# A four-layer graph network on one core: four packed adjacency buffers instead of two, and a tenth of x made per chunk

## The chip, the cores and the metric

The kernel is one program on one core of a Trainium2 chip. The metric is device time in microseconds from start to end of one execution, as the median of three executions: 19903.77 us, between 19867.3 and 19942.51. The engines are called as in the profile: PE is the matmul engine and PEld its weight loads, DVE the vector engine, ACT the activation engine, POOL the gather engine, SP the queue that issues the large transfers.

## The reference, cut to what matters

The graph has 12500 nodes with 32 features and 412500 directed edges. Four graph layers follow each other, each added to its input and normalised over the features. The change touches layers 2 and 3, which are both repeated products with the same adjacency matrix:

```python
# layer 2: ten steps of personalised propagation
f = feat0 = x
for _ in range(10):
    agg = segment_sum((f * src_norm)[src], dst)      # adjacency @ f
    f = 0.9 * (agg * dst_norm) + 0.1 * feat0         # feat0 = x, ALPHA = 0.1
x = layernorm(x + f)
# layer 3: one product more
x = layernorm(x + segment_sum(x[src], dst))
```

Layer 1 (an edge network with means) runs before it, layer 4 (tensor messages on every edge) behind it.

## The kernel before

The adjacency matrix is dense and lies in HBM as small counts, two of them packed in each byte (a nibble each) in planes; `planes` says how many planes hold anything, and it is 1 here. `propagate` makes 11 passes over the matrix: passes 0 to 9 are the ten steps of layer 2, pass 10 is layer 3.

One pass has NCH = 14 chunks of output nodes, walked in pairs: `c2` counts the 7 pairs, and m = 0 or 1 is the chunk in the pair. A chunk needs HG = 7 slots of the matrix (h = 0 to 6), so a pair has SLOTS = 14 tiles (j = 0 to 13), a pass has 98, and the stage has 11 x 98 + 7 = 1085, since the load of the next pass's first chunk is also made once at the very end. Each tile takes these steps:

- SP, `load` (L1151): waits until the packed buffer is free (a count in `a_unpacked`), then issues one transfer of 784 KB into `packed[j % 2]`, one of two buffers. L1151 is the only transfer of the stage.
- DVE, `unpack` (L1287, L1288): waits for the landing and for PE to be through with the old content of slot `j % 7` (`a_used`), then writes the low and the high nibbles into the slot with two instructions.
- PE, `product` (L1206): 84 pairs of a weight load and a matmul over the slot. There are 7 slots in SBUF, so DVE can be at most one whole chunk ahead of PE.

Behind the first slot of each product (`TURN_AFTER = 1`), PE turns back the product of the chunk before (`turn_back`, L1186, 14 small matmuls) from what ACT copied out (L1246). DVE, having unpacked the 7 slots of the next chunk, adds the turned product to `agg` (`add`, L1294) and runs `finish`: `new_f` scales `agg`, adds the stored tenth of x (L1319, `tenth`, written once at L1351 before the first pass) and clears `agg` (L1322); `next_parts` then splits the new f into three bf16 parts for the next pass (L1328, L1274, L1277). Pass 9 has the shorter `finish` `into_x` (L1336), pass 10 has none.

What sets the order: SP, PE and DVE each run a `Fori` loop whose body is one pair. PE's body is written out, 2 x 588 matmuls with their weight loads and two `turn_back`s. PE has three copies of the code of a pass: even passes (source `parts[0]`), odd passes (`parts[1]`), and pass 10. In each copy the first pair is peeled off, and the other six go round the `Fori`, so the jump back to the top happens 5 times in a pass, and once more when the outer loop over two passes goes round. SP has one copy of `load_plane` for each of the 5 planes, and jumps over four of them in each pass.

`tenth` serves also as scratch for the two layer norms inside the stage (`norm(3, ...)`, `norm(4, ...)`).

Of the kernel before, what the change touches and what calls it, by code (L numbers as in the profile page):

```python
# [31 lines left out]
P = 128  # L32
# [1063 lines left out]


TURN_AFTER = 1


def propagate(nc, k, s):
# [4 lines left out]
    sb, pb, sem = k.sb, k.pb, k.sem  # L1106
    passes = STEPS + 1
    slots = [sb(f"a_slot{h}", [P, 4, HH, QW], U8, s) for h in range(HG)]
    packed = [sb(f"a_nibbles{n}", [P, 4 * PW_H], U8, s) for n in range(2)]
    parts = [sb(f"f_parts{t}", [P, NB, 3 * D], BF16, s) for t in range(2)]  # L1110
    agg = sb("agg", [P, NB, D], F32, s)
    chunk_f = sb("chunk_f", [P, CB * D], F32, s)
    chunk_zero = sb("chunk_zero", [P, CB * D], F32, s)
    tenth = sb("x_tenth", [P, NB, D], F32, s)
    norms = sb("norms", [P, NB, 2], F32, s)
    mean, var = sb("mean", [P, NB], F32, s), sb("var", [P, NB], F32, s)
    turned = sb("turned", [P, 2, CW], F32, s)
# [11 lines left out]
    with ExitStack() as q:  # L1129
        prod = [pb(f"p_prod{m}", [P, 2, 512], F32, q) for m in range(2)]  # L1130
        back = [pb(f"p_back{m}", [P, CB * D], F32, q) for m in range(2)]
        with nc.Block() as block:
# [9 lines left out]
            @block.sync  # L1142
            def _(sp):
                planes = sp.value_load(k.ctl[0:1, 1:2], min_val=1, max_val=DIGITS)
                u = sp.alloc_register("pairs_sp")
                sp.reg_mov(u, 0)

                def load(plane, chunk, n, j):

                    await_alone(sp, k.passed_sp, a_unpacked, n * SLOTS + (j + 1))  # L1150
                    sp.dma_start(view(packed[j % 2][:], 0, [[PW_H, 4], [1, PW_H]]),  # L1151
                                 slot_part(plane, chunk, j % HG)).then_inc(a_loaded[j], 16)

                def load_plane(d):
                    with sp.Fori(0, NCH // 2) as c2:
                        n = sp.snap(u, min_val=0, max_val=passes * DIGITS * NCH)
                        for j in range(SLOTS):
                            load(k.planes[d], c2 * 2 + j // HG, n, j)
                        sp.reg_add(u, u, 1)
                with sp.Fori(0, passes):  # L1160
                    load_plane(0)
                    for d in range(1, DIGITS):
                        with sp.If(planes > d):
                            load_plane(d)
                n = sp.snap(u, min_val=0, max_val=passes * DIGITS * NCH)
                for j in range(HG):
                    load(k.planes[0], 0, n, j)
                sp.wait_ge(x_ready, 1)
                sp.dma_start(k.x3_d.rearrange("(b p) f -> p b f", p=P), k.x[:]).then_inc(x_stored, 16)
                sp.wait_ge(x_stored, 16)  # L1170

            @block.tensor
            def _(pe):
# [15 lines left out]

                def product(n, m, source, p=None, turn_after=TURN_AFTER):  # L1190

                    if turn_after == 0:
                        turn_back(n, m)
                    pe.wait_ge(product_copied, n * 2 + (m + 1))
                    for h in range(HG):
                        if p is not None:
                            await_alone(pe, k.passed_pe, parts_ready, p * HG + (h + 1))
                        await_alone(pe, k.passed_pe, a_unpacked, n * SLOTS + (HG * m + h + 3))
                        for j in range(HH):
                            for r in range(3):  # L1200
                                for w in range(2):

                                    unit = (h * HH + j) * 3 + r
                                    strip = unit % 2 * 2 + (w + unit // 2) % 2
                                    rows = slice(strip * D, (strip + 1) * D)
                                    mm = nc.tensor.matmul(view(prod[m][rows, w, :], 0, [[QW, 2], [1, QW]]),  # L1206
                                                          source[:, h * HH + j, r * D:(r + 1) * D],
                                                          slots[h][:, 2 * w:2 * w + 2, j, :].bitcast(FP8),
                                                          start=(unit < STRIPS), stop=(unit >= NB * 3 - STRIPS),
                                                          tile_position=(0, strip * D))  # L1210
                        mm.then_inc(a_used, 1)
                        if h + 1 == turn_after:
                            turn_back(n, m)
# [41 lines left out]
            def _(dve):  # L1255
# [2 lines left out]
                u = dve.alloc_register("pairs_dve")  # L1258
                dve.reg_mov(u, 0)
                dve.sem_inc(taken, 3)  # L1260
                dve.sem_inc(a_unpacked, 2)
                for r in range(STRIPS):
                    nc.vector.tensor_copy(select[r * D:(r + 1) * D, :], k.ident[r * D:(r + 1) * D, r * D:(r + 1) * D])
                for d in range(DIGITS):
# [12 lines left out]
                            tt(frm, frm, to(r), ALU.subtract)  # L1277
                            dve.drain()

                def unpack(n, j, ahead=0):  # L1280

                    await_alone(dve, k.passed_dve, a_loaded[j], n * 16 + (16 + 16 * ahead))
                    await_alone(dve, k.passed_dve, a_used, n * SLOTS + (SLOTS * ahead + j + 1))
                    words = PW_H // 4
                    frm = view(packed[j % 2][:].bitcast(I32), 0, [[words, 4], [1, words]])
                    half = lambda i: view(slots[j % HG][:].bitcast(I32), i * words, [[2 * words, 4], [1, words]])
                    ts(half(0), frm, NIBBLES, None, ALU.bitwise_and)  # L1287
                    ts(half(1), frm, 4, NIBBLES, ALU.logical_shift_right, ALU.bitwise_and).then_inc(a_unpacked, 1)  # L1288
# [7 lines left out]
                def one_pass(finish):  # L1296

                    with dve.Fori(0, planes) as d:
                        with dve.Fori(0, NCH // 2) as c2:
                            n = dve.snap(u, min_val=0, max_val=passes * DIGITS * NCH)  # L1300
                            for m in range(2):
                                for h in range(HG):
                                    unpack(n, (1 - m) * HG + h, m)
                                add(n, m, c2)
                                if finish is not None:
                                    with dve.If(planes - d == 1):
                                        finish(c2 * 2 + m)
                                        if finish is not into_x and m == 1:
                                            dve.drain().then_inc(parts_ready, 1)
                            dve.reg_add(u, u, 1)  # L1310

                def new_f(c):
# [2 lines left out]
                    dve.drain()  # L1315
                    tt(view(agg[:], c * (CB * D), [[D, CB], [1, D]]), view(agg[:], c * (CB * D), [[D, CB], [1, D]]),
                       view(norms[:], c * (2 * CB), [[2, CB], [0, D]]), ALU.mult)
                    dve.drain()
                    nc.vector.scalar_tensor_tensor(chunk_f[:], part, 1.0 - ALPHA, view(tenth[:], c * (CB * D), [[1, CB * D]]),  # L1319
                                                   ALU.mult, ALU.add)  # L1320
                    dve.drain()
                    nc.vector.tensor_copy(part, chunk_zero[:])  # L1322

# [20 lines left out]

                norm(1, agg)
                for h in range(2):
                    unpack(0, h)
                ts(norms[:], k.small[:], 1.0, None, ALU.max).then_inc(norm_in, 1)
                dve.wait_ge(norm_out, 2)
                nc.vector.reciprocal(norms[:], norms[:])  # L1350
                ts(tenth[:], k.x[:], ALPHA, None, ALU.mult)  # L1351
                dve.drain()
                tt(agg[:], k.x[:], of_src, ALU.mult)
                all_parts()
                dve.drain().then_inc(parts_ready, HG)
                for h in range(2, HG):
                    unpack(0, h)
                with dve.Fori(0, STEPS // 2 - 1):
                    for odd in range(2):
                        one_pass(next_parts(parts[1 - odd]))  # L1360
                one_pass(next_parts(parts[1]))
                one_pass(into_x)
                dve.drain()
                norm(3, tenth)
                nc.vector.tensor_copy(agg[:], k.x[:])
                all_parts()
                dve.drain().then_inc(parts_ready, HG)
# [1 line left out]
                dve.drain()  # L1369
                tt(k.x[:], k.x[:], agg[:], ALU.add)  # L1370
                dve.drain()
                norm(4, tenth)
                dve.drain().then_inc(x_ready, 1)


# [420 lines left out]
```

## Time and profile before

| | us |
|---|---|
| median of three executions | 19903.77 |
| lowest, highest | 19867.3, 19942.51 |
| the profiled execution, its own time | 19936.66 |
| its span, first to last instruction | 19934.9 |
| before the adjacency stage | 8342 |
| prologue of the stage (norms, first parts) | 48 |
| passes 0 to 9 | 4603 |
| between pass 9 and pass 10 | 44 |
| pass 10 | 448 |
| behind it (layer 3's norm, layer 4) | 6449 |

All other durations in this document come from the profiled execution. In the profile's page the busy tenths of PE are at 9 in slices 17 to 26 of 40, each 498 us long; that is the adjacency stage. DVE is there at 4 to 5 tenths, the transfers at 5 tenths and 170 to 178 GB/s. In an answer on a stretch of instructions in order of time, the columns are start, duration, engine, line, operation, what it writes and reads, the count of merged instructions, and in brackets the idle time before it with what ended it; "issue" means that the engine waited for nothing that the profile shows. The DMA section lists, for each queue, packets, megabytes and the share of 16 engines' time; a queue named "instruction" carries program code to an engine's sequencer.

### The profile page before, as it was taken

What the parts mean: (1) busy time and instruction counts of PE and PEld (TensorE: products, weight loads), DVE (VectorE), ACT (ScalarE), POOL (GpSimd) and SP (SyncE); (2) the same over time, 40 slices, a digit from 0 to 9 for tenths busy, and PEclk for the clock granted to TensorE, in tenths of its full rate; (3) what the DMA queues carried; (4) which work ended last, traced back from release to release, by engine and by line L of the source; (5) the groups of instructions that cost most, each with busy time, mean ns of one, the idle gap of its engine ahead of it and who ended that gap; (6) DMA issues with size and microseconds to landing.
All of it is one profiled execution on the core that took longest, in us unless ns stands there. A gap on an engine that the chain in (4) does not pass through costs nothing. (4 is left out here: it accounts for less than half of the span.)

```text
span 19934.9 us, 398915 instructions
## 1 busy us (share of the span) xinstructions
PE 14773.5 (74%) x139606; PEld 9691.4 (49%) x139607; DVE 10952.7 (55%) x15417; ACT 5231.4 (26%) x10549; POOL 7485.0 (38%) x8530
## 2 busy tenths in 40 slices
PE   3666666666666666699999999986777777777787
PEld 2555555555555555355555555553444444444444
DVE  6444444444443444354555555446777777777777
ACT  2333333332333333000000000003444444444443
POOL 4343343433443442000000000005666666666665
PEclk8666666666666666699999999998999999999999
DMA  2010000000000000155555555551111111111111
GB/s 71 19 23 19 22 20 21 20 22 20 22 22 20 23 20 23 40 178 171 176 171 174 172 172 177 173 163 38 27 27 27 27 27 27 27 26 27 27 28 27
DMA packets 1144165, 1253.76 MB, mean 63 GB/s; under 512 B 399195, under 2 KB 1111895, under 8 KB 1142455
## 3 DMA queue, kind: packets, MB, share of 16 engines
q1 hardware_dynamic: 932547, 1124.29, 18.7%
q0 software_dynamic: 210496, 113.01, 3.9%
q8 instruction: 887, 14.53, 0.3%
q14 instruction: 235, 1.93, 0.0%
HBM read 1143.04 MB, written 93.60 MB: 62 GB/s over the span
## 5 line engine op out<-in xcount | busy, mean ns | idle before, releaser
L1458 POOL DMA_INDIRECT m_src<-x_after_layer,m_idx x3240 | 3164.0, 977 | 6734.6 <-DMA m_idx<-in_src 5620.8
L180 POOL DMA_INDIRECT l_xin<-in_x,l_idx x3240 | 3076.0, 949 | 4605.8 <-DMA l_idx<-in_src 3416.8
L1206 PE MATMUL p_prod<-a_slot,f_parts 128*32 128x448 fp8e4 x90552 | 4475.0, 360 | 418.2 <-issue 283.6
L1206 PEld LDWEIGHTS p_prod<-a_slot,f_parts 128*32 128x32 bf16 x90552 | 2460.3, 99 | 2370.3 <-issue 608.1
L581 PE MATMUL a_ps<-hot_hi,hot_lo 128*128 128x196 bf16 x6272 | 1645.0, 304 | 2122.3 <-ACT a_image L680 1034.4
L1589 PE MATMUL radial_ps<-radial_w,radial_hidden 128*128 128x384 f32 x6480 | 2621.1, 542 | 706.2 <-DVE m_products L1728 425.3
L749 DVE TENSOR_TENSOR hot_hi<-window_hi,number_ps 128x1568 bf16<-128x1568 f32 x784 | 1401.3, 1787 | 2985.2 <-PE degree_ps L582 1532.7
L1594 PE MATMUL m_visit_ps<-m_products,m_onehot 128*128 128x288 f32 x8420 | 2471.8, 444 | 640.1 <-DVE m_onehot L1695 287.6
L1594 PEld LDWEIGHTS m_visit_ps<-m_products,m_onehot 128*128 128x128 f32 x8420 | 1685.5, 203 | 1455.5 <-issue 842.6
L1589 PEld LDWEIGHTS radial_ps<-radial_w,radial_hidden 128*128 128x128 f32 x6480 | 1228.8, 205 | 1990.3 <-issue 764.2
L680 ACT ACTIVATE a_image<-a_ps 128x392 fp8e4<-128x392 f32 x3136 | 1477.6, 496 | 2691.0 <-PE a_ps L581 1509.3
L1287 DVE TENSOR_SCALAR a_slot<-a_nibbles 128x1568 int32<-128x1568 int32 x1085 | 1059.3, 976 | 1691.4 <-DMA a_nibbles<-multiplicity_digit 1308.6
L581 PEld LDWEIGHTS a_ps<-hot_hi,hot_lo 128*128 128x128 bf16 x6272 | 722.8, 115 | 2543.0 <-issue 1259.0
L1724 DVE TENSOR_TENSOR m_products<-radial_ps,m_features 128x512 f32<-128x512 f32 x1620 | 1113.7, 687 | 1203.8 <-PE radial_ps L1589 442.7
L1728 DVE TENSOR_TENSOR m_products<-radial_ps,m_features 128x256 f32<-128x256 f32 x4860 | 1745.6, 415 | 0.0
L582 PE MATMUL degree_ps<-hot_hi,hot_lo 128*128 128x196 bf16 x6272 | 1664.3, 307 | 17.0 <-issue 17.0
L1561 ACT ACTIVATE m_difference<-m_nodes,m_dst 128x128 f32 x3240 | 981.9, 388 | 2529.1 <-PEq L1614 1407.8
L622 PE MATMUL e_visit_ps<-e_onehot,e_hidden 128*97 x8420 | 1364.2, 334 | 312.1 <-ACT e_hidden L693 152.0
L622 PEld LDWEIGHTS e_visit_ps<-e_onehot,e_hidden 128*97 128x97 f32 x8420 | 1310.7, 216 | 380.2 <-issue 373.0
L1246 ACT ACTIVATE turned<-p_prod,digit_weight 128x896 f32<-128x896 f32 x154 | 155.2, 1008 | 4941.0 <-PE p_prod L1206 4941.0
L611 PE MATMUL h_ps<-w1a,xt 49*128 49x96 f32 x6480 | 1257.5, 357 | 237.5 <-issue 122.3
L611 PEld LDWEIGHTS h_ps<-w1a,xt 49*128 49x128 f32 x6480 | 1121.5, 259 | 424.8 <-issue 424.8
(202 smaller groups left out, 12633.2 us busy)
## 6 DMA issues: line engine op xcount, KB each, us to landing
a_nibbles<-multiplicity_digit SPq DMA_DIRECT2D x1085, 784.0 KB, 4.5
edge_w<-in_edge_weight SPq DMA_DIRECT2D x324, 320.0 KB
multiplicity_digit<-a_packed SPq DMA_DIRECT2D x392, 196.0 KB
l_xin<-in_x,l_idx POOLq DMA_INDIRECT x3240
m_src<-x_after_layer,m_idx POOLq DMA_INDIRECT x3240
xt<-in_edge_attr SPq DMA_DIRECT2D x324, 80.0 KB, 2.1
edge_directions<-rel_unit SPq DMA_DIRECT2D x12, 675.0 KB
m_unit<-edge_directions SPq DMA_DIRECT2D x324, 25.0 KB
```

What stands on the lines that cost most here:

```text
L180: pool.indirect_dma_start(k.xin[m][:, j, :], None, k.io["x"], bass.IndirectOffsetOnAxis(k.idx[m][:, j:j + 1], 0)).then_inc(k.gathered[m], 16)
L581: counts = nc.tensor.matmul(a_ps[:, bank, v * WC:(v + 1) * WC], lo, hot_hi[batch % 2][:, w, :], start=True, stop=True)
L582: mm = nc.tensor.matmul(degree_ps[:, 0:WC], lo, hot_hi[batch % 2][:, w, :], start=False, stop=False, skip_group_check=True)
L611: mm = nc.tensor.matmul(h_ps[:, t * DH:(t + 1) * DH], xt[:, m % 2, (b * HT + t) * EP:(b * HT + t + 1) * EP], w1a[:], start=True, stop=True)
L622: mm = nc.tensor.matmul(visit_ps[:, 0:P], hid[m % 2][:, j, :], view(onehot[:], (v % 2) * (G * P) + j * P, [[1, P]]), start=(j == 0), stop= ...
L680: nc.scalar.activation(view(image[:], h * (NB * QW) + 4 * l, [[QW, NB], [1, 4]]).bitcast(FP8), view(a_ps[:], l % 2 * 512, [[1, NB], [NB, 4 ...
L749: tt(hot_hi[b % 2][:], view(k.window_hi[:, bass.ds(at, WB)], 0, [[1, WB], [0, WC]]), view(numbers, 0, [[0, WB], [1, WC]]), ALU.is_equal)
L1206: mm = nc.tensor.matmul(view(prod[m][rows, w, :], 0, [[QW, 2], [1, QW]]), source[:, h * HH + j, r * D:(r + 1) * D], slots[h][:, 2 * w:2 * ...
L1458: pool.indirect_dma_start(src[m][:, j, :], None, k.x3_d, bass.IndirectOffsetOnAxis(idx[m][:, j:j + 1], 0)).then_inc(gathered[m], 16)
L1589: mm = nc.tensor.matmul(r_ps[:, half, t, 0:RD], hid[m][:, b * RB + t, :], w2[:], start=True, stop=True)
L1594: mm = nc.tensor.matmul(view(v_ps[:], (v % 3) * 512, [[U + 1, D], [1, U + 1]]), onehot[one][:, j, :], view(prod[m][:], j * PW + FIRST, [[R ...
L1728: mul = tt(view(prod[m][:], t0 * PW + LONG + o * U * RW + 1, [[PW, RB], [RW, U], [1, 2 * U]]), view(r_ps[:], at + 4 * U * U, [[512, RB], [ ...
```

## The change

The two packed buffers become one tensor `a_nibbles` with room for AHEAD = 4 tiles. Since 14 tiles of a pair is not a multiple of 4, tile j of pair n lies at place j mod 4 where n is even, and at that place moved by two where n is odd; SP and DVE compute the offset from the pair's parity, which they keep in a register (`odd`, `even`), so the address of the packed tile is no longer a constant. Each wait on `a_unpacked` allows two tiles more. `tenth` goes; `new_f` makes the tenth of its chunk from `k.x` in `chunk_f` with one instruction, and the norms use `agg` as scratch. The four buffers take 25088 bytes a partition instead of 12544, which `tenth` (12544 bytes) gives back.

```diff
+AHEAD = 4
+def packed_at(odd, j):
+    at = j % AHEAD
+    return (at + 2 * odd if at < 2 else at - 2 * odd) * PW_H
...
-    packed = [sb(f"a_nibbles{n}", [P, 4 * PW_H], U8, s) for n in range(2)]
+    packed = sb("a_nibbles", [P, AHEAD * 4 * PW_H], U8, s)
-    tenth = sb("x_tenth", [P, NB, D], F32, s)
...
-                def load(plane, chunk, n, j):
+                def load(plane, chunk, n, odd, j):
                     await_alone(sp, k.passed_sp, a_unpacked, n * SLOTS + (j + 1))
-                    sp.dma_start(view(packed[j % 2][:], 0, [[PW_H, 4], [1, PW_H]]),
+                    sp.dma_start(view(packed[:], packed_at(odd, j) * 4, [[PW_H, 4], [1, PW_H]]),
                                  slot_part(plane, chunk, j % HG)).then_inc(a_loaded[j], 16)
...
                         n = sp.snap(u, min_val=0, max_val=passes * DIGITS * NCH)
+                        odd = sp.snap(n % 2, min_val=0, max_val=1)
...
-                        await_alone(pe, k.passed_pe, a_unpacked, n * SLOTS + (HG * m + h + 3))
+                        await_alone(pe, k.passed_pe, a_unpacked, n * SLOTS + (HG * m + h + AHEAD + 1))
...
-                dve.sem_inc(a_unpacked, 2)
+                dve.sem_inc(a_unpacked, AHEAD)
...
-                def unpack(n, j, ahead=0):
+                def unpack(n, odd, j, ahead=0):
...
-                    frm = view(packed[j % 2][:].bitcast(I32), 0, [[words, 4], [1, words]])
+                    frm = view(packed[:].bitcast(I32), packed_at(odd, j), [[words, 4], [1, words]])
...
+                            odd = dve.snap(n % 2, min_val=0, max_val=1)
+                            even = dve.snap((n + 1) % 2, min_val=0, max_val=1)
                             for m in range(2):
                                 for h in range(HG):
-                                    unpack(n, (1 - m) * HG + h, m)
+                                    unpack(n, even if m else odd, (1 - m) * HG + h, m)
...
+                    ts(chunk_f[:], view(k.x[:], c * (CB * D), [[1, CB * D]]), ALPHA, None, ALU.mult)
                     dve.drain()
-                    nc.vector.scalar_tensor_tensor(chunk_f[:], part, 1.0 - ALPHA, view(tenth[:], c * (CB * D), [[1, CB * D]]),
-                                                   ALU.mult, ALU.add)
+                    nc.vector.scalar_tensor_tensor(chunk_f[:], part, 1.0 - ALPHA, chunk_f[:], ALU.mult, ALU.add)
...
-                ts(tenth[:], k.x[:], ALPHA, None, ALU.mult)
...
-                norm(3, tenth)
+                norm(3, agg)
...
-                norm(4, tenth)
+                norm(4, agg)
```

## Rows read from the trace of the kernel before

**Rows 1.** Busy time by stretch: stretch, us, then each engine's busy us, PEclk, DMA, GB/s.
```profile
8390.40:12993.30 4602.90, 4295.43 (x84280) 2463.13 (x84280) 2307.37 (x3293) 140.09 (x139) 0.00 (x0) 0.96 0.56 174
13485.30:19934.00 6448.70, 5015.79 (x14904) 2915.44 (x14904) 4896.26 (x9084) 2651.88 (x5186) 4308.82 (x5184) 0.92 0.14 27
```
**Rows 2.** PE in order of time, around one jump back in pass 1.
```profile
9215.75 24.02 PE L1206 MATMUL p_prod<-a_slot,f_parts 128*32 128x448 fp8e4 x504
9244.15 0.57 PE L1206 MATMUL p_prod<-a_slot,f_parts 128*32 128x448 fp8e4 x4 [4.39 <-DVE a_slot L1288]
9246.92 5.70 PE L1206 MATMUL p_prod<-a_slot,f_parts 128*32 128x448 fp8e4 x80 [2.20 <-issue]
...
9254.23 27.99 PE L1206 MATMUL p_prod<-a_slot,f_parts 128*32 128x448 fp8e4 x588
```
**Rows 3.** Groups of instructions in that trip of the loop, 9186.1 to 9254.2 us.
```profile
L1206 PE MATMUL p_prod<-a_slot,f_parts 128*32 128x448 fp8e4 x1176 | 58.3, 360 | 6.6 <-DVE a_slot L1288 4.4 <-issue 2.2
...
L1287 DVE TENSOR_SCALAR a_slot<-a_nibbles 128x1568 int32<-128x1568 int32 x14 | 13.7, 976 | 20.7 <-DMA a_nibbles<-multiplicity_digit 19.7 <-issue 1.0
...
L1322 DVE COPY agg<-chunk_zero 128x224 f32 x2 | 0.6, 277 | 0.1
```
**Rows 4.** DMA queues in the same stretch: packets, MB, share of 16 engines.
```profile
q8 instruction: 12, 0.20, 1.2%
```
**Rows 5.** Waits in the whole stage, 8391 to 13483 us: total us, times, longest.
```profile
DVE a_slot L1287 <- DMA a_nibbles<-multiplicity_digit: 1308.6, 629, 4.7
```
**Rows 6.** PE: where passes 0, 1, 8 and 9 come behind their first slot.
```profile
8397.79 27.99 PE L1206 MATMUL p_prod<-a_slot,f_parts 128*32 128x448 fp8e4 x588
...
8854.75 27.99 PE L1206 MATMUL p_prod<-a_slot,f_parts 128*32 128x448 fp8e4 x588
...
12083.86 27.99 PE L1206 MATMUL p_prod<-a_slot,f_parts 128*32 128x448 fp8e4 x588
...
12537.72 27.99 PE L1206 MATMUL p_prod<-a_slot,f_parts 128*32 128x448 fp8e4 x588
```
**Rows 7.** PE behind one jump back in an even pass, pass 0.
```profile
8583.94 2.43 PE L1206 MATMUL p_prod<-a_slot,f_parts 128*32 128x448 fp8e4 x23 [4.63 <-issue]
8586.64 3.99 PE L1206 MATMUL p_prod<-a_slot,f_parts 128*32 128x448 fp8e4 x61 [0.26 <-issue]
```
**Rows 8.** The last pass: DVE's unpack and PE around one jump back.
```profile
13222.58 0.98 DVE L1287 TENSOR_SCALAR a_slot<-a_nibbles 128x1568 int32<-128x1568 int32 x1 [2.11 <-PE p_prod L1206]
...
13226.13 5.84 PE L1206 MATMUL p_prod<-a_slot,f_parts 128*32 128x448 fp8e4 x84 [3.71 <-issue]
```
**Rows 9.** PE in pass 9: two trips, and what follows one later jump back.
```profile
12732.77 27.99 PE L1206 MATMUL p_prod<-a_slot,f_parts 128*32 128x448 fp8e4 x588
...
12800.05 27.99 PE L1206 MATMUL p_prod<-a_slot,f_parts 128*32 128x448 fp8e4 x588
...
12857.50 0.37 PE L1206 MATMUL p_prod<-a_slot,f_parts 128*32 128x448 fp8e4 x4 [3.83 <-issue]
12862.13 5.45 PE L1206 MATMUL p_prod<-a_slot,f_parts 128*32 128x448 fp8e4 x80 [4.26 <-issue]
...
12869.19 1.13 PE L1206 MATMUL p_prod<-a_slot,f_parts 128*32 128x448 fp8e4 x20
...
12931.41 6.64 PE L1206 MATMUL p_prod<-a_slot,f_parts 128*32 128x448 fp8e4 x80 [3.98 <-issue]
```
**Rows 10.** DMA queues from 9244.4 to 9245.4 us, pass 1.
```profile
q8 instruction: 1, 0.02, 6.1%
```
**Rows 11.** DMA queues, pass 9: 12857.7 to 12859.7 us, then 12859.5 to 12861 us.
```profile
q1 hardware_dynamic: 443, 0.68, 96.7%
...
q8 instruction: 1, 0.02, 4.2%
```
**Rows 12.** DVE in the prologue of the stage.
```profile
8368.72 1.73 DVE L1351 TENSOR_SCALAR x_tenth<-x 128x3136 f32<-128x3136 f32 x1
```
**Rows 13.** DMA queues from 9276.3 to 9286.3 us, while SP crosses from pass to pass.
```profile
q14 instruction: 4, 0.03, 1.0%
```

## What the change does to the time: a prediction

> **What bounds the kernel now.** I read the busy time by stretch first. In passes 0 to 9 PE is busy 4295.4 of 4602.9 us and DVE 2307.4 [rows 1]. The change works in this stretch and the 500 us around it; layer 4, 6449 us, has no line of it. So the question is what PE waits for in the 307 us that it is idle, and whether it has anything to do with packed buffers.
>
> Then PE in order of time [rows 2]. A chunk is 588 matmuls in 27.99 us and 14 small ones, 29.6 us in all, with no idle time. Every second chunk it breaks off: 504 matmuls, 4.39 us idle, 4 matmuls, 2.20 us idle, 80 matmuls in 5.70 us. The break stands between slots 6 and 0, at the point where the pair's loop jumps back, and it comes once in a pair. The releaser named there (DVE's unpack) is a coincidence: the slot that PE wants was unpacked almost a chunk earlier, since DVE ran seven tiles in that chunk before the break ended. PE is waiting for its own program. One trip holds 1176 matmuls and as many weight loads [rows 3], and the queue that carries code moves 12 packets, 0.20 MB, in it [rows 4]: the code of the loop is brought in again on each trip. In straight code that goes on unseen beside the matmuls; at the jump PE waits for the target, then for the next 16 KB block: behind 4 matmuls in odd passes [rows 2], behind 23 in even ones [rows 7]. Pass 10 has no second wait in its first slot [rows 8]. After the pause the matmuls run at half the granted clock at first: 84 take 5.84 us [rows 8] where six slots take 24.02, 4.0 each [rows 2].
>
> DVE waits 1308.6 us in 629 waits for the landing of a tile [rows 5]. That is what the change is about, and it ends nobody's idle time: DVE is a chunk ahead of PE, and nothing on PE's own path is late for data.
>
> **How large the breaks are.** I take PE's start behind the first slot of a pass. Pass 0 to pass 1: 8854.75 - 8397.79 = 457.0 us; pass 0 to pass 8: 3686.07 us, or 921.5 for an even and an odd pass; pass 8 to 9: 453.9 [rows 6]. Fourteen undisturbed chunks are 14 x 29.6 = 414.4. So an even pass loses (455 - 414.4) / 5 = about 8.1 us a jump. The pair loses 921.5 - 828.8 = 92.7; less 40.5, and less some 5.5 for the outer loop's jump (the form of rows 8), an odd pass loses 46.7 / 5 = 9.3 a jump. Over the stage these breaks are some 530 us, and the only thing in the change that can touch them is the traffic that the code packets meet. The PE code of the change differs from the old one only in the constant of one wait, so I take the places of the blocks as they are.
>
> **Part 1, two buffers more.** Today, in passes 0 to 8, DVE unpacks two tiles, then waits for transfers whose times follow DVE, not PE. With four buffers a tile lies ready whenever PE frees a slot. DVE is busy 2307.4 / 140 = 16.5 us a chunk [rows 1], PE needs 29.6, so DVE makes up the 5 to 6 us of its `finish` at 2 us a slot (4.0 less two instructions of 0.98 [rows 3]) and is waiting for PE from the fourth slot on. That state is in the trace already: pass 10, which has no `finish`, shows DVE released by PE at each slot [rows 8], and the last trips of pass 9, with its short one, are alike. Then a load is issued some 2 us behind each slot that PE ends, so around the jump the transfers stand at fixed times: one runs over the fetch of the target, the next over the fetch of the second block. The rows show both cases. In pass 1 the second code packet runs in the us from 9244.4, that is 4.6 to 5.6 us after PE stopped at 9239.8 [rows 2, 10]. In pass 9, from 12857.7 to 12859.7, 4.0 to 6.0 us after the stop, the nibble queue fills 96.7% of the engines and no code packet is there; it comes in the next stretch [rows 11]. PE's second wait is 4.26 us there, against 2.20 [rows 2, 9].
>
> Odd passes: that trip took 12869.19 - 12800.05 = 69.14, 9.9 above 59.2. The trip before it, which was not yet in step, took 67.28, 8.1 above [rows 9]. A later one has 80 matmuls in 6.64 instead of 5.45 [rows 9], so up to 11.1. I take 10.3 for a trip in step: 20 jumps (passes 1, 3, 5, 7) x (10.3 - 9.3) = +20 us, and for two trips of pass 9 that fall into step, 2 x 2.2 = +4.
>
> Even passes: no row shows one in step, so it is bounded. First wait 3.8 as in rows 9, 23 matmuls at the slow clock 2.43 [rows 7], so 6.2; the block that ends the second wait at 3.83 + 0.37 + 4.26 = 8.5 in rows 9 ends this one too; then 61 matmuls, from 4.4 (61 x 5.45 / 80, plus a little) to 5.8 (the same 5.84 as a whole slow slot). Together 12.9 to 14.3, less 4.0: 8.9 to 10.3. I take 9.6, the middle: 25 x (9.6 - 8.1) = +37. The lower end without any collision is the 8.1 of rows 9's first trip or a bit less, say 7.0 where the second wait is short as in rows 7: 25 x -1.1 = -28.
>
> The outer jumps and pass 10 are already in the state of rows 8: 0 to +1. PE's wait constant and DVE's 1308.6 us of waiting: nothing on the path.
>
> **Part 2, the moving address.** SP and DVE get register instructions before a transfer or an unpack. They lie beside a DVE that is idle 13 us a chunk and in front of buffers that are full. Where that cover is gone, 0.1 us a tile x 1078 would be 108 us; it is not gone while PE sets the pace. I take 0.
>
> **Part 3, the tenth.** In the prologue DVE is alone on the path, and the 1.73 us of L1351 go [rows 12]: -1.7. In each of 140 chunks one instruction on 128x224 is added; the nearest in size is L1322 at 277 ns [rows 3]. 140 x 0.28 = 39 us on DVE, all in its spare time but one: behind the last chunk of pass 9 PE waits for the norm of layer 2, +0.3. `agg` as scratch changes no instruction.
>
> **Sum:** 20 + 4 + 37 + 1 - 1.7 + 0.3 = +61 us. Against the profiled execution that is 19936.7 + 61 = 19998. This execution lies 33 us above the median of the three, within their spread, and nothing in the sum depends on it, so on the median I forecast 19903.8 + 61 = 19965 us. A measurement of this kernel can tell about 0.5% from no change, so this is within "the same".
>
> **Rivals.**
>
> The breaks don't care: loads in step with PE are elsewhere by luck, the even passes' gain takes up the odd ones' loss, or the four buffers don't bring DVE into step because transfers come one at a time. Time 19902. Against it: 629 waits for landing follow a pair of unpacks, and pass 9 came into step with two buffers.
>
> The breaks get shorter: if DVE draws its tiles early in the chunk and the queue is quiet at the jump, code packets meet nothing: 20 x (8.1 - 9.3) + 25 x (7.0 - 8.1) = -52, 19850. For it: code comes fastest where nothing else moves. Against it: 14 tiles a pair are 11 MB whatever the number of buffers, and a full queue of buffers can only take one tile for each slot that PE frees, the last of them at the jump itself.
>
> Slower, by program size: SP and DVE also fetch their code. Crossing from one pass to the next, SP jumps over four copies of its loop, and in those 10 us there are four code packets on its kind of queue [rows 13], 2.5 us each. The added register instructions, some 2 for each of 14 tiles in each copy, lengthen these loops and shift DVE's later code, the loop of layer 4 among it, against the blocks. If that loop (162 trips; DVE is busy 4896 of 6449 us there [rows 1]) came to need two blocks again on each trip, 162 x 2 x 2.5 = 810 us, of which DVE's idle quarter may hide a part: 300 to 810, so 20200 to 20710. It decides from 0.6 us a trip. Against it: DVE's trip in this stage fetches nothing today. The Trainium skill (Advanced Engine Details and Errata, "ISA Cache") gives 32 KB for such an engine and 128 KB for TensorE, in lines of 16 KB. By it PE's trip, 2352 instructions of 64 bytes, does not fit, as the 12 packets of rows 4 agree, while DVE's loops would still fit; the same page's "Only 2 cache lines" is what speaks for this rival, and no run here has tried it.
>
> **The chances.** Forecast mechanism 0.50, 19965, its own range 19925 to 20030 (the upper end with 11.1 for all 45 jumps, 45 to 75 us more than the middle). Breaks don't care 0.27. Shorter 0.19. Program size 0.04. Slower by over 0.5% means above 20003: a quarter of the forecast and the last rival, 0.16. Faster by over 0.5%, below 19804: the tail of the shorter breaks, 0.04. The range 19855 to 20025 leaves out that tail, the program-size rival and the top of the forecast.
>
> **What would show it.** In the profile after: DVE's waits for landing fall from 1308 us to under 200 and its waits for PE rise in their place; PE's chunks stay at 27.99 + 1.75. At the jumps the first wait is near 3.8 us everywhere; the second is 4.2 in odd passes and near 2.2 in even ones; code packets come 6 us after the stop. A trip in odd passes takes 69.5, in even ones 68.8. The prologue is 1.7 us shorter. I am wrong if the second waits stay as they are or shrink, if PE's blocks fall elsewhere (other counts than 4 and 23), or if code packets turn up in layer 4.

## The result, and the profile after

The changed kernel takes 20010.27 us, the median of ten executions, beside 19915.31 us for ten of the kernel before. One of the changed kernel's ten took 38941.94 us at a mean granted clock of 0.376, where the others had 0.83; the ratio leaves it out, and the median of the other nine is 20006.46 us. The ratio is 1.004, with a 95% interval from 1.0027 to 1.0054: a small loss of some 80 us. The forecast was +61 us and 19965 us, in a range from 19855 to 20025.

The profiled execution has a span of 19937.7 us against 19934.9, which hides the loss: its first matmul of the adjacency stage stands at 8337.35 us, not at 8390.40, since the layers before, which the change does not touch, took 53 us less in this execution. Stretch by stretch the loss is there. PE in order of time, at the places of [rows 6] (the columns are start, duration, engine, line, operation; L1214 is the old L1206):

```profile
8345.35 27.99 PE L1214 MATMUL p_prod<-a_slot,f_parts 128*32 128x448 fp8e4 x588
...
8807.29 27.99 PE L1214 MATMUL p_prod<-a_slot,f_parts 128*32 128x448 fp8e4 x588
...
12087.06 27.99 PE L1214 MATMUL p_prod<-a_slot,f_parts 128*32 128x448 fp8e4 x588
...
12548.22 27.99 PE L1214 MATMUL p_prod<-a_slot,f_parts 128*32 128x448 fp8e4 x588
```

Passes 0 to 7 take 12087.06 - 8345.35 = 3741.7 us where they took 3686.1: 13.9 us more for an even and an odd pass. A chunk itself is unchanged at 27.99. From first to last matmul of the stage it is 69.5 us more, 5160.8 against 5091.3.

The waits of the stage (engine and line, whom it waited for, total us, times, longest), to be read against [rows 5]:

```profile
DVE a_slot L1295 <- PE p_prod L1214: 1207.6, 645, 7.4
...
PE p_prod L1214 <- issue: 446.7, 110, 40.4
```

and the same groups before:

```profile
DVE a_slot L1287 <- PE p_prod L1206: 304.0, 145, 7.5
PE p_prod L1206 <- issue: 283.6, 90, 40.5
PE p_prod L1206 <- DVE a_slot L1288: 83.9, 20, 5.1
```

After the change there is no line for DVE waiting on a transfer: the 1308.6 us are gone. They came back as waits for PE, 1207.6 us for 304.0 here, and the rest where DVE waits for the turned product, 1126.7 us for 710.7. PE, which sets the pace, waits longer for its own program: 446.7 us for 283.6 + 83.9 = 367.5, the second term being the waits that are put down to DVE by coincidence. The change did what it says, and on an engine that had time to spare. The same jump back of the loop, in an odd and in an even pass:

```profile
8993.41 0.37 PE L1214 MATMUL p_prod<-a_slot,f_parts 128*32 128x448 fp8e4 x4 [3.83 <-issue]
8997.84 5.35 PE L1214 MATMUL p_prod<-a_slot,f_parts 128*32 128x448 fp8e4 x80 [4.06 <-issue]
...
9004.80 27.99 PE L1214 MATMUL p_prod<-a_slot,f_parts 128*32 128x448 fp8e4 x588
```

```profile
8600.28 1.46 PE L1214 MATMUL p_prod<-a_slot,f_parts 128*32 128x448 fp8e4 x23 [3.86 <-issue]
8604.89 4.79 PE L1214 MATMUL p_prod<-a_slot,f_parts 128*32 128x448 fp8e4 x61 [3.15 <-issue]
```

The first wait is 3.8, and the second 4.06 where [rows 2] has 2.20; in even passes it is 3.15 where [rows 7] has 0.26. One jump isn't the average, though. Over the 20 jumps of odd passes the first wait is 4.38 us in the mean before and 4.09 after, the second 2.41 and 3.83; over the 25 of even passes the first is 3.82 and 3.92, the second 1.07 and 2.73 (all read from PE's timeline). So in the mean the first wait moved by 0.3 us down and 0.1 up; what the change added inside the passes is in the second. The DMA queues say why. PE stopped at 8989.6 (8993.41 - 3.83). From 8993.6 to 8995.6 us, 4 to 6 us after the stop, and then from 8995.5 to 8996.9:

```profile
q1 hardware_dynamic: 456, 0.70, 97.2%
...
q1 hardware_dynamic: 36, 0.03, 7.0%
q8 instruction: 1, 0.02, 4.3%
```

A tile's transfer fills the engines for two us, and the code packet starts when it is through, as in [rows 11]. And DVE is in step with PE from the fourth slot of a chunk on, here in the chunk before that jump:

```profile
8978.02 0.98 DVE L1295 TENSOR_SCALAR a_slot<-a_nibbles 128x1568 int32 x1 [1.66 <-PE p_prod L1214]
...
8981.81 0.98 DVE L1295 TENSOR_SCALAR a_slot<-a_nibbles 128x1568 int32 x1 [1.93 <-PE p_prod L1214]
...
8985.78 0.98 DVE L1295 TENSOR_SCALAR a_slot<-a_nibbles 128x1568 int32 x1 [2.11 <-PE p_prod L1214]
...
8989.76 0.98 DVE L1295 TENSOR_SCALAR a_slot<-a_nibbles 128x1568 int32 x1 [2.11 <-PE p_prod L1214]
```

The last of these stands 0.2 us behind PE's stop; the load that it makes room for goes out 2 us later and is on the queue when the second block of code is asked for.

### The profile page after: what moved, and what is told of

Its sections match the earlier page's. It is cut to its first block and busy times, and to the rows that moved or that the text cites. A ratio compares the mean times of both kernels' runs of the same rounds, so it can differ in the third digit from the quotient of the medians.

```text
span 19937.7 us, 400278 instructions
## 1 busy us (share of the span) xinstructions
PE 14768.4 (74%) x139606; PEld 9677.8 (49%) x139607; DVE 10957.9 (55%) x15556; ACT 5228.0 (26%) x10549; POOL 7476.6 (37%) x8530
## 5 line engine op out<-in xcount | busy, mean ns | idle before, releaser
L1214 PE MATMUL p_prod<-a_slot,f_parts 128*32 128x448 fp8e4 x90552 | 4465.2, 359 | 496.3 <-issue 446.7
L1214 PEld LDWEIGHTS p_prod<-a_slot,f_parts 128*32 128x32 bf16 x90552 | 2455.1, 98 | 2444.4 <-issue 678.3
L1295 DVE TENSOR_SCALAR a_slot<-a_nibbles 128x1568 int32 (+1 forms) x1085 | 1057.8, 975 | 1337.9 <-PE p_prod L1214 1229.0
```

## The experiments

The theory: once DVE is in step with PE, the loads issued around the jump back stand at fixed times that fall on both code fetches, and each collision adds to PE's wait. The means above say that the first fetch met loads before the change too. The rivals: the register instructions and the chunk's own tenth cost it; more queued transfers cost it in proportion; the code fetch takes its time whatever else moves, and the difference lies in code places.

One measure serves for all runs: the loss a jump, the mean distance between PE's starts behind the first slot over two chunks, less 59.2 us. It comes from the same lines as [rows 6] and [rows 9], over all 25 jumps of even passes, 20 of odd passes (without pass 9), the 4 outer ones and the 5 of pass 10. The ratio is that to the kernel before, run on the same chip. The runs from "one load held" on were made on two other chips, "one load held" and "before, PE's code shifted" on one and the rest on the other; the kernel before took 19639 and 19637 us there. There is no trace of the kernel before or the changed kernel from either, so only ratios and losses are compared across chips, and a loss within some 0.5 us.

| kernel | ratio, 95% interval | even | odd | outer | pass 10 |
|---|---|---|---|---|---|
| before | 1 | 8.1 | 9.2 | 5.5 | 5.9 |
| changed | 1.0040 (1.0027 to 1.0054) | 9.4 | 10.5 | 7.2 | 5.8 |
| changed, two tiles ahead | 1.0016 (1.0004 to 1.0027) | 8.7 | 8.9 | 6.3 | 5.8 |
| changed, three tiles ahead | 1.0048 (1.0032 to 1.0064) | 9.5 | 10.6 | 7.5 | 5.8 |
| two loads held at the jump | 0.9965 (0.9950 to 0.9980) | 6.2 | 7.6 | 5.2 | 3.9 |
| two loads held elsewhere | 1.0041 (1.0029 to 1.0053) | 9.4 | 10.6 | 7.4 | 6.1 |
| one load held, the second | 1.0001 (0.9987 to 1.0015) | 7.5 | 9.2 | 8.1 | 5.3 |
| the tenth alone | 1.0004 (0.9990 to 1.0018) | 7.6 | 8.9 | 5.1 | 5.7 |
| a seventh of each tile | 0.9973 (0.9958 to 0.9988) | 6.4 | 7.8 | 5.0 | 3.7 |
| PE's code shifted | 0.9931 (0.9915 to 0.9947) | 5.7 | 5.8 | 7.8 | 5.8 |
| before, PE's code shifted | 0.9917 (0.9896 to 0.9938) | 5.9 | 5.1 | 5.0 | 5.8 |
| shifted, two loads held | 0.9856 (0.9839 to 0.9874) | 3.6 | 3.5 | 5.4 | 3.3 |

**Depth taken away by a constant.** Everything of the change stays, but SP may be only two tiles ahead.

```diff
-                    await_alone(sp, k.passed_sp, a_unpacked, n * SLOTS + (j + 1))
+                    await_alone(sp, k.passed_sp, a_unpacked, n * SLOTS + (j + 3))
```

> The changed kernel with one constant different: SP may again be only two tiles ahead. Moving addresses, four places and the chunk's own tenth stay. My theory (loads that run in step with PE meet the code packets behind the jump back): the loads follow DVE again as in the kernel before, the loss per jump falls from 9.35 us (even passes) and 10.5 us (odd) to about 8.1 and 9.3, outer jumps from 7.2 to 5.5, so about 65 us less than the changed kernel: near 19915 us, ratio to the kernel before 1.000. Rival 1 (the register instructions and the tenth cost it): it stays at 1.004, near 20000 us, and the losses per jump stay at 9.4 and 10.5. Rival 2 (half and half): 1.002.

Ratio 1.0016. DVE's waits in the stage are again for transfers:

```profile
DVE a_slot L1295 <- DMA a_nibbles<-multiplicity_digit: 1196.6, 562, 5.0
DVE a_slot L1295 <- PE p_prod L1214: 437.8, 212, 7.7
```

and in an odd pass the second wait is back at 2.2 us:

```profile
9016.58 0.57 PE L1214 MATMUL p_prod<-a_slot,f_parts 128*32 128x448 fp8e4 x4 [4.72 <-DVE a_slot L1296]
9019.37 5.50 PE L1214 MATMUL p_prod<-a_slot,f_parts 128*32 128x448 fp8e4 x80 [2.22 <-issue]
```

The odd passes are where they were or below (8.9 against 9.2); the even ones stay 0.6 us above the kernel before. The stage is 12.9 us longer than before, of the 69.5: so most of the loss hangs on the depth alone, and rival 1, that the register instructions and the tenth cost it, falls. The second wait of even passes is 1.89 us in the mean, between the 1.07 before and the 2.73 after; why it isn't all the way back no run tells. The ratio fits neither expectation fully, nearer to the half-way case; what is left of it, 8 to 54 us by the interval, takes in the 13 us of the stage, and whether there is more isn't told.

**Three tiles ahead**, with `j + 2` in the same place.

> The changed kernel with SP allowed three tiles ahead. My theory: what counts is not how much is buffered but whether DVE comes into step with PE before the jump. A load is landed 4.5 us after its issue; with three places the tile for the fourth slot is issued when DVE's first unpack of the chunk ends, some 5 us before it is wanted, so DVE is in step: the same as with four, losses of 9.4 and 10.5 us a jump, ratio 1.003 to 1.004. Rival (each buffer more means more queued transfers in front of the code packets): halfway, losses of 8.7 and 9.9, ratio 1.002.

Ratio 1.0048, losses 9.5 and 10.6: as large as with four. DVE waits for transfers only 117 times, 202.7 us in all. It isn't how much is queued; it is whether DVE reaches PE's pace before the jump, which three places do.

**Two loads held at the jump.** Tiles 9 and 10 of a pair wait until tile 7 is unpacked.

```diff
-                    await_alone(sp, k.passed_sp, a_unpacked, n * SLOTS + (j + 1))
+                    await_alone(sp, k.passed_sp, a_unpacked, n * SLOTS + (HG + 1 + AHEAD if j in (9, 10) else j + 1))
```

> The changed kernel, but the loads of tiles 9 and 10 of a pair, which it issues some 2 us before and 2 us behind the jump, wait until DVE has unpacked tile 7, some 18 us behind the jump; nobody needs them sooner. Same transfers, same buffers. My theory: both code fetches then meet an empty queue. The first wait falls from 3.8 to some 3 us (packet at 0.2 instead of 1.1 us), the second from 4 to about 2.2 (packet at 3.4 instead of 6.1): losses of 7 to 7.8 us a jump in both kinds of pass, 45 jumps x 2 to 3 us plus pass 9, outer jumps and pass 10, so 110 to 160 us less than the changed kernel: 19850 to 19900, ratio 0.994 to 0.998, faster than both. Rival (the code fetch takes its time whatever else moves; the longer waits of the changed kernel come from something else, such as code places): 1.004 and unchanged losses.

Ratio 0.9965, the profiled stage 169 us shorter than that of the changed kernel. In an odd pass the waits are 2.64 and 2.08 us, and in the 8 us from PE's stop at 8954.0 the queues hold two code packets and next to nothing else:

```profile
8956.68 0.56 PE L1214 MATMUL p_prod<-a_slot,f_parts 128*32 128x448 fp8e4 x4 [2.64 <-DVE a_slot L1296]
8959.32 5.74 PE L1214 MATMUL p_prod<-a_slot,f_parts 128*32 128x448 fp8e4 x80 [2.08 <-issue]
```

```profile
q8 instruction: 2, 0.03, 1.5%
q1 hardware_dynamic: 6, 0.01, 0.3%
```

The same bytes, buffers and instructions, moved in time, take the whole loss away and more. This is the run that decides between traffic and code places as the source of the difference. The first wait is 2.8 us in the mean, below the 3 expected. DVE now waits 348.6 us for transfers again behind the hold, and it costs PE nothing.

**Two loads held elsewhere**, the control: tiles 2 and 3 until tile 0 is unpacked (`1 + AHEAD if j in (2, 3) else j + 1`), at the chunk border in the middle of the loop body.

> The control to the run that holds two loads at the jump: here tiles 2 and 3 of a pair are held in the same way, until tile 0 is unpacked. They belong to the other chunk border, in the middle of PE's loop body, where there is no jump. My theory: no effect, losses of 9.4 and 10.5 us a jump, ratio 1.004. Rival (holding loads helps by thinning or bunching traffic in general): as much faster as the run held at the jump.

Ratio 1.0041, losses unchanged within 0.3 us. Holding as such does nothing.

**One load held.** Only tile 10 (`if j == 10`), so that the load over the first fetch stays.

> The changed kernel with only the load of tile 10 held until tile 7 is unpacked, the one that is issued 2 us behind the jump. The load of tile 9, issued 2 us before it, stays. My theory (two separate collisions, one for each code fetch): the first wait stays at 3.8 to 4.2 us, the second falls from some 3.9 to some 2.2 in odd passes; losses of about 7.7 (even) and 8.7 us (odd), pass 10 unchanged at 5.8 since it has no second wait; ratio 0.999 to 1.001. Rival (one collision only, the first delays the whole chain of fetches): losses stay near 9.4 and 10.5.

```profile
8838.80 0.37 PE L1214 MATMUL p_prod<-a_slot,f_parts 128*32 128x448 fp8e4 x4 [3.77 <-issue]
8841.31 6.53 PE L1214 MATMUL p_prod<-a_slot,f_parts 128*32 128x448 fp8e4 x80 [2.14 <-issue]
```

The first wait stays at 3.77, the second is 2.14: there are two collisions, and each can be taken away by itself. The second one costs 1.3 to 1.9 us a jump (9.4 to 7.5, 10.5 to 9.2), the first about as much again (7.5 to 6.2, 9.2 to 7.6), across two chips. Odd passes came down less than expected, by 1.3 and not 1.8, and the outer jumps got dearer, 8.1 for 7.2: in three of the four the slot behind the wait takes 6.7 to 7.0 us, and no run tells why.

**The tenth alone**, two buffers and constant addresses.

```diff
-    tenth = sb("x_tenth", [P, NB, D], F32, s)
...
+                    ts(chunk_f[:], view(k.x[:], c * (CB * D), [[1, CB * D]]), ALPHA, None, ALU.mult)
                     dve.drain()
-                    nc.vector.scalar_tensor_tensor(chunk_f[:], part, 1.0 - ALPHA, view(tenth[:], c * (CB * D), [[1, CB * D]]),
-                                                   ALU.mult, ALU.add)
+                    nc.vector.scalar_tensor_tensor(chunk_f[:], part, 1.0 - ALPHA, chunk_f[:], ALU.mult, ALU.add)
```

> The kernel before with the second half of the change alone: no stored tenth, one more instruction for each chunk, the norms on agg; two buffers with constant addresses. My theory: the prologue is 1.7 us shorter, 140 added instructions of 0.28 us lie in DVE's spare time; ratio 1.000, losses per jump near 8.1 and 9.2 us. Rival (DVE's later finish delays the loads and moves them against the jump): losses differ by some 0.5 us a jump, ratio up to 1.0015, which would also explain what is left at a depth of two.

Ratio 1.0004, from 0.9990 to 1.0018: no difference that can be told. The losses are not above those of the kernel before, so the rival finds no support; the interval alone doesn't rule its 1.0015 out.

**A seventh of each tile.**

```diff
-                    sp.dma_start(view(packed[:], packed_at(odd, j) * 4, [[PW_H, 4], [1, PW_H]]),
-                                 slot_part(plane, chunk, j % HG)).then_inc(a_loaded[j], 16)
+                    sp.dma_start(view(packed[:], packed_at(odd, j) * 4, [[PW_H, 4], [1, QW]]),
+                                 slot_part(plane, chunk, j % HG)[:, :, 0:QW]).then_inc(a_loaded[j], 16)
...
+                nc.vector.memset(packed[:], 0)
+                dve.drain()
                 dve.sem_inc(a_unpacked, AHEAD)
```

It leaves six sevenths of the matrix out: those parts of the buffers are zeros.

> The changed kernel with a seventh of each tile transferred (112 KB for 784), in place of the full tile; the rest of the buffers is zeroed once, which adds some 6 us to the prologue, so six sevenths of the matrix are left out of the result. Same number of transfers, same waits, same PE work. My theory: a transfer takes a fraction of a us on the queue and code packets meet next to nothing: losses of about 6 us (even), 7.5 (odd) and 3.9 (pass 10), as where the two loads were held, ratio 0.996 to 0.997. Rival 1 (holding only took part of the collisions away): clearly below these losses. Rival 2 (the losses are not a matter of traffic): 9.4 and 10.5.

Ratio 0.9973, losses 6.4, 7.8 and 3.7 us, those of the two held loads within 0.2. DVE is in step with PE here and the number of transfers is the same; what differs is their length, and the zeros that PE multiplies. So holding two loads took away nearly all that traffic costs, and the rest, 6 to 8 us a jump, is PE's fetch in an empty queue plus the slow start behind it:

```profile
8845.15 0.37 PE L1214 MATMUL p_prod<-a_slot,f_parts 128*32 128x448 fp8e4 x4 [2.91 <-DVE a_slot L1298]
8848.26 6.65 PE L1214 MATMUL p_prod<-a_slot,f_parts 128*32 128x448 fp8e4 x80 [2.74 <-issue]
```

**PE's code shifted.**

```diff
+                for _ in range(56):
+                    pe.sem_inc(k.passed_pe, 1)
                 pe.sem_inc(a_used, HG)
```

> The changed kernel with 56 semaphore increments that nobody waits for put in front of PE's passes. By the counts of matmuls between the jump and the second wait (23 and 4) the block border then falls behind the first slot in both copies of the loop, as in pass 10. No transfer and no wait changes. My theory (the second wait is for the second block of code): it goes; losses near 5.8 us in both kinds of pass as in pass 10, 25 x 3.6 + 25 x 4.7 = about 205 us less than the changed kernel, near 19800 us, ratio 0.993 to 0.995. The outer jumps may gain a second wait, 4 times 2 us. Rival (the second wait comes from something else at the start of a slot, a queue or a clock): still 9.4 and 10.5.

```profile
8810.47 5.84 PE L1216 MATMUL p_prod<-a_slot,f_parts 128*32 128x448 fp8e4 x84 [3.85 <-issue]
```

Ratio 0.9931. The slot behind the jump is whole, one wait, and the losses of 5.7 and 5.8 are those of pass 10. The second wait is for the next block of code, and 56 increments that nobody waits for take it away. The outer jumps went from 7.2 to 7.8 us, as the expectation allowed. The shift alone is worth more than the whole change costs.

**The same shift in the kernel before.**

> The kernel before, two buffers, with the same 56 increments in front of PE's passes. My theory: the second wait goes here too, what is left is one fetch at the jump, met by loads at changing times: losses near 5.8 us in both kinds of pass, so 25 x 2.3 + 25 x 3.5 = about 145 us less than the kernel before, ratio 0.992 to 0.994. Then the third and fourth buffer cost nothing any more, since their price lay in the second fetch: the changed kernel shifted in the same way stood at 0.993. Rival (four buffers cost their 70 us whatever the code places): 0.9895 to 0.991.

Ratio 0.9917, losses 5.9 and 5.1. The ratio lies between the theory's 0.992 and the rival's 0.991 and its interval takes in both. The losses say more: the expectation holds for even passes; in odd ones and at the outer jump the kernel with two buffers stays 0.6 and 2.8 us better, so the added buffers still cost something. The profiled stages differ by 21.7 us (4930.9 and 4952.6), a third of the 69.5 without the shift: two thirds of the price of the added buffers lay in the second fetch, as far as one profile each, on two chips, can tell; the two ratios' intervals overlap.

**Both: shifted, and two loads held.**

> The changed kernel with both: PE's code shifted by 56 increments, and the loads of tiles 9 and 10 held until tile 7 is unpacked. My theory: one fetch a jump is left and it meets no transfer, as in pass 10 of the run held at the jump (3.85 us): losses near 3.9 in all passes, 25 x 2.4 + 25 x 3.7 = about 150 us less than held alone, near 19685 us, ratio 0.988 to 0.990, the fastest of all. Rival (the two remedies take away the same wait): no better than the better of the two alone.

```profile
8824.26 4.16 PE L1216 MATMUL p_prod<-a_slot,f_parts 128*32 128x448 fp8e4 x84 [2.42 <-DVE a_slot L1298]
```

Ratio 0.9856, the fastest of all, 1.8% below the changed kernel's ratio and below the 0.988 to 0.990 expected. The ratios of the two remedies add up (1.0040 - 0.0075 - 0.0109 = 0.9856); in the profiled stages they fall 35 us short of it (5160.8 - 169.2 - 208.2 = 4783.4, measured 4818.2, across two chips). The losses of 3.6 and 3.5 are below the 3.9 expected because behind some waits, as behind the 2.42 us here, the slot takes 4.16 us, not 5.84 (the last section shows the clock). Of the 4818.2 us, 259.8 are left beyond 154 x 29.6, and 44.7 of those are the norm between pass 9 and pass 10.

## Why the prediction was right, point by point

**What bounds the kernel** held: PE's own pace and PE's fetch of its program at the jump. That 1308 us of DVE waits could vanish and the kernel still not gain is the plain proof. One figure there was read too large: of the "some 530 us" of breaks, some 45 are the norm between pass 9 and pass 10, so the jumps are some 487. The sum doesn't use it.

**Part 1, in step:** most of the signs named came: waits for landing from 1308.6 us to none, waits for PE 1207.6 us in their place, the second code packet some 6 us behind the stop, trips of 69.7 us in odd passes and 68.6 in even ones for the 69.5 and 68.8 named. The first waits inside the passes are 3.66 to 4.65 us, so "near 3.8 everywhere" was a little low; the second waits of odd passes are 3.83 in the mean for 4.2, and the two misses nearly cancel. The terms: odd passes 10.5 where I took 10.3, so 20 x (10.5 - 9.2) = 26 us for my 20. Even passes 9.4 where I took 9.6, so 25 x (9.4 - 8.1) = 31 for my 37, both from rounded losses. The sign that failed is the second wait there, 2.73 us in the mean (3.15 in the jump shown) and not 2.2, because the 23 matmuls in front of it ran in 1.90 us in the mean (1.46 there), not the 2.43 that I took. The end of that wait is the same, some 8.5 us behind the stop, since 3.86 + 1.46 + 3.15 = 8.5 and the means give 3.92 + 1.90 + 2.73 = 8.55, and it was the right thing to work from. Pass 9: 5 x (10.7 - 9.35) = 7 for my 4.

**The term mis-sized** is the outer jump, "0 to +1": it went from 5.5 to 7.2, four times, so +6.5 us. I took it for the form of pass 10 [rows 8] because it too has no second wait. But before the change it wasn't in the state of pass 10; no load delayed its fetch. Before, then after, then with both loads held and the code shifted, then with only tile 10's load held:

```profile
9311.40 5.84 PE L1206 MATMUL p_prod<-a_slot,f_parts 128*32 128x448 fp8e4 x84 [3.56 <-issue]
...
9273.89 5.75 PE L1214 MATMUL p_prod<-a_slot,f_parts 128*32 128x448 fp8e4 x84 [5.35 <-issue]
...
9074.80 5.81 PE L1216 MATMUL p_prod<-a_slot,f_parts 128*32 128x448 fp8e4 x84 [3.40 <-issue]
...
9113.72 7.04 PE L1214 MATMUL p_prod<-a_slot,f_parts 128*32 128x448 fp8e4 x84 [5.15 <-issue]
```

Over the four outer jumps the first wait is 3.56 to 3.83 us before, 5.35 to 5.48 after, 5.15 to 6.07 with tile 9's load left in place and 3.32 to 3.79 with both held and the code shifted (with both held alone, 3.29 to 3.58 in three and 4.52 in one). So the price of the outer jump is the load of tile 9, issued 2 us before the jump, on the first fetch. The queues agree. Before, the code packet is on the queue within 1.4 us of PE's stop at 9307.8:

```profile
q8 instruction: 1, 0.02, 5.7%
```

After, for 2 us from the stop at 9268.5 there are only packets of the tile, and the code comes in the next stretch, to 9271.8:

```profile
q1 hardware_dynamic: 452, 0.70, 96.8%
...
q8 instruction: 1, 0.02, 5.0%
```

**Part 2, the moving address,** 0: with two tiles ahead the addresses stay and the ratio is 1.0016. The 13 us in the stage bound what they and the tenth cost there in sum, by one profile; nothing splits them. **Part 3:** the prologue from DVE's first unpack to PE's first matmul is 26.0 us for 27.2, so 1.2 us shorter where L1351 alone had 1.73 [rows 12]; 0.5 us of it went into a pause behind the first cast. The added instruction is 0.27 us:

```profile
8966.78 0.27 DVE L1328 TENSOR_SCALAR chunk_f<-x 128x224 f32 x1
```

**Sum:** 26 + 31 + 7 + 6.5 = 70.5 us, of which pass 10 and the norm in front of it give 1 back: the 69.5 measured in the stage. Less 1.2 for the prologue it is 68, for the 61 forecast. The interval of the ratio is 54 to 108 us; the 12 us between 68 and its middle lie outside the stage or in the spread, and no run tells which. The parts inside the passes were missed by 3 to 6 us each in both directions, so that the sum came as close as it did is in part luck. Of the 45 us between 19965 and 20010, 12 are the kernel before itself, whose median over ten executions is 19915 and not 19904.

**The rivals.** Breaks that don't care: refuted by the two held loads and their control. Shorter breaks: they would have come if the loads had fallen elsewhere, as the run with held loads shows, but four buffers by themselves put them on the fetches (the second above all). Program size: layer 4 shows no code packets on each trip. From 13600 to 19900 us there are four in all, where layer 4 has some 158 trips (6300 us of the 6449 in which it makes 162). The Trainium skill (Advanced Engine Details and Errata, "ISA Cache") has room for DVE's loops and none for PE's, and these two counts and the 12 packets a trip of [rows 4] agree.

```profile
q8 instruction: 2, 0.03, 0.0%
q14 instruction: 2, 0.02, 0.0%
```

## What to carry to other kernels

Before adding buffers, ask which engine's wait ends last: 1300 us of waiting for data were worth nothing here, since the engine that waited was a chunk ahead. Deeper prefetch also fixes the time at which transfers go out, so look at what else uses the queue then; here two loads issued some 2 us before and behind the jump, or both some 21 us behind it, are the difference between 1.004 and 0.9965. A matmul engine's loop that is written out too long to stay loaded pays at each jump back; look for a queue of code packets on each trip and for waits at the top of the loop that nobody releases, place its head near the start of a block and keep the queue empty there. A body small enough to stay loaded would be the other way; it was not tried here.

## What the runs showed of the hardware that was not expected

PE's wait for the target of a jump inside a pass is 2.3 to 3.1 us where no transfer runs (with the code shifted and both loads held), and 3.6 to 4.3 where one does (with the code shifted alone). At the outer jump it is 3.3 to 3.8 and 5.1 to 5.4 in the same two runs.

The pause can also cost a second time, through the clock. Stretches behind a jump (stretch, us, then busy us of PE, PEld, DVE, ACT, POOL, the granted clock, DMA share, GB/s), first with the code shifted and a wait of 3.85 us:

```profile
8812.00:8813.50 1.50, 1.50 (x24) 0.79 (x17) 0.00 (x0) 0.00 (x0) 0.00 (x0) 0.50 0.40 144
...
8815.00:8816.30 1.30, 1.30 (x29) 0.65 (x21) 0.00 (x0) 0.00 (x0) 0.00 (x0) 1.00 0.00 0
```

then shifted with the two loads held, behind 2.42 us:

```profile
8825.50:8827.00 1.50, 1.50 (x40) 0.96 (x35) 0.00 (x0) 0.00 (x0) 0.00 (x0) 1.00 0.00 0
```

At 0.50, the 1.2 GHz level, 24 matmuls go through in 1.5 us; at 1.00, 2.4 GHz, 40 do. The whole slot took 5.84 us in the one and 4.16 in the other. It isn't so at each jump: in the run with both remedies, over the 55 jumps inside passes, pauses of 2.31 to 3.06 us were followed by a slot of 4.16 us 31 times, and pauses of 2.32 to 2.98 us by one of 5.82 to 5.84 us 19 times, and nothing here tells which it will be. One of the latter, behind 2.60 us:

```profile
8392.50:8394.00 1.50, 1.50 (x23) 0.79 (x16) 0.00 (x0) 0.00 (x0) 0.00 (x0) 0.50 0.00 0
```
